# Weights that share an address between layers, one level of a scan folded into another, and loops written out

## The reference, cut to what matters

```
# layer 2, per sample (32 heads of 16), xa = layer norm of x, sx = previous token's xa - xa
xxx = tanh((xa + sx * maa_x) @ maa_w1).reshape(l, 5, 32)
xxx = einsum('lfd,fde->lfe', xxx, maa_w2)
xk, xw, xv, xr, xg = xa + sx * (maa_stack + xxx)
w = exp(-exp(time_decay + tanh(xw @ td_w1) @ td_w2))
r, k, v, g = xr @ Wr.T, xk @ Wk.T, xv @ Wv.T, silu(xg @ Wg.T)
for t: a = k_t v_t;  out_t = r_t (u * a + s);  s = a + w_t * s
x1 = x + groupnorm(out) * g @ Wo.T
x2 = x1 + sigmoid(xr2 @ Wfr.T) * (relu(xk2 @ Wfk.T) ** 2 @ Wfv.T)
# layer 3: q = x2 @ Wq, k and v from the context, softmax attention, @ Wo, layer norm
```

## Time and profile before

| | |
|---|---|
| median of 3 runs | 2489.3 us (2488.08 to 2489.41) |
| the profiled execution's own time | 2494.95 us |
| its span, first to last instruction | 2492.6 us |
| PE busy | 2331.0 us, 94% |
| DVE, ACT, POOL busy | 45%, 43%, 22% |
| mean granted PE clock | 0.966 |
| DMA | 81.93 MB, mean 33 GB/s |

### The profile page before, as it was taken

The page is one execution under the profiler, slowest core; times in us unless marked ns, Lnnn a source line. Parts: engine busy times, 40 slices in busy tenths (PEclk is TensorE's granted clock), DMA queues, the critical chain, the costliest instruction groups (busy, mean ns, idle before and its releaser), DMA issues. The chain is left out here.

```text
span 2492.6 us, 59022 instructions
## 1 busy us (share of the span) xinstructions
PE 2331.0 (94%) x22880; PEld 1720.1 (69%) x22880; DVE 1111.1 (45%) x3070; ACT 1082.6 (43%) x3409; POOL 552.4 (22%) x585
## 2 busy tenths in 40 slices
PE   7886999999999999999488999999999999999986
PEld 3444667777777666667276878777777877777864
DVE  5662222222222222222234565655666655665542
ACT  4552333333333333333112655555555455555544
POOL 0001010110000000000023334333333343343320
PEclk9997999999999999999678999999999999999998
DMA  5421000000000000000600000111000011100010
GB/s 165 168 89 65 15 18 18 22 18 18 18 18 18 18 18 18 18 10 5 191 15 16 21 17 14 25 25 25 20 20 12 23 25 25 25 20 16 10 25 14
DMA packets 117056, 81.93 MB, mean 33 GB/s; under 512 B 79136, under 2 KB 91680, under 8 KB 114720
## 3 DMA queue, kind: packets, MB, share of 16 engines
q1 hardware_dynamic: 107744, 54.32, 8.2%
q0 software_dynamic: 2240, 12.58, 1.5%
q10 hardware_dynamic: 6912, 12.59, 1.3%
HBM read 62.68 MB, written 12.58 MB: 30 GB/s over the span
## 5 line engine op out<-in xcount | busy, mean ns | idle before, releaser
L745 PEld LDWEIGHTS bank<-normedT,mlp_w 128*128 128x128 f32 x2048 | 235.7, 193 | 18.3 <-issue 17.1
L745 PE MATMUL bank<-normedT,mlp_w 128*128 128x128 f32 x2048 | 241.7, 278 | 0.8 <-DVE normedT L975 0.8
L755 PE MATMUL bank<-mlp_w,geluT 128*128 128x512 f32 x512 | 228.9, 595 | 0.0
L1638 PEld LDWEIGHTS quad<-rT,k_even_odd 32*128 32x128 f32 x6144 | 187.2, 193 | 39.5 <-DVE wkv_scores L2095 29.7
L926 DVE CUSTOM_DVE_ANT_0 probs<-quad,neg_mask 128x256 f32<-128x256 f32 x256 | 90.8, 421 | 273.8 <-PE quad L675 273.8
L1638 PE MATMUL quad<-rT,k_even_odd 32*128 32x32 f32 x6144 | 197.9, 278 | 13.9 <-DVE wkv_scores L2095 11.5
L2095 DVE COPY_PREDICATED wkv_scores<-level_masks,quad 128x1024 f32<-128x1024 int32 x96 | 160.6, 1673 | 93.4 <-PE quad L1638 93.4
L1930 ACT ACTIVATE scores<-scores,nmax 128x128 f32<-128x128 f32 x512 | 198.9, 400 | 2.9 <-DVE nmax L2185 2.9
L933 DVE COPY probsT<-quad 128x512 f32<-128x512 f32 x128 | 84.9, 683 | 191.9 <-PE quad L689 191.7
L755 PEld LDWEIGHTS bank<-mlp_w,geluT 128*128 128x128 f32 x512 | 93.6, 190 | 103.4 <-issue 103.4
L1445 POOL TENSOR_TENSOR k_even_odd<-k_even_odd,decay_products 128x512 f32<-128x512 f32 x80 | 95.9, 1199 | 275.9 <-PE quad L1638 275.9
(11 more groups left out here) (238 smaller groups left out, 4463.7 us busy)
## 6 DMA issues: line engine op xcount, KB each, us to landing
x_in<-in_x SPq DMA_DIRECT2D x32, 256.0 KB, 3.0
mlp_w<-in_mlp_w POOLq DMA_DIRECT2D x8, 1024.0 KB, 5.5
ctx_in<-in_ctx SPq DMA_DIRECT2D x16, 256.0 KB, 2.9
l_out<-wy ACTq DMA_DIRECT2D x16, 256.0 KB, 2.2
wy_in<-l_out SPq DMA_DIRECT2D x16, 256.0 KB, 3.4
hT<-in_ctxT SPq DMA_DIRECT2D x16, 256.0 KB, 3.5
l_out<-l_x ACTq DMA_DIRECT2D x16, 256.0 KB, 2.0
x_in<-l_out SPq DMA_DIRECT2D x16, 256.0 KB, 3.0
```

Source lines behind the costliest of these rows:

```text
L745: mm = nc.tensor.matmul(PS[b][:, f * P:(f + 1) * P], mlp_w1[:, c, m * P:(m + 1) * P], nT[:, c, :], start=(c == 0), stop=(c == NC - 1))
L755: mm = nc.tensor.matmul(PS[M.bank][:, :], gT[:, f, :], mlp_w2[:, f, :], start=(f == 0), stop=(f == NF - 1))
L1638: mm = nc.tensor.matmul(PS[r][:, at:at + SB], keys(rr, c, s), odd, start=True, stop=True)
```

## The change

Four things change.

1. **Shared weights.** `Wk`, `Wr`, `Wv` and the raw `Wg` get the addresses of layer 1's `q_w`, `k_w`, `v_w` and `out_w`, and SP loads them in layer 1 as soon as the last sample's output projection is done. `Wo3` gets the address of the raw `Wg` once that is reordered. The other weights are loaded by ACT's queue at the start of `layers23`. Zeros, constants, the centring of `Wv` (DVE) and the reordering of `Wg` (now POOL) move behind step 0.
2. **The bonus level.** `p_diag` goes. Level 0 computes it too: keys are `K0`, in which the odd tokens carry u and the even ones don't (`p_k0` of POOL), queries are `rm`, in which even tokens carry u (`p_ur`), 64 moving columns. The merge of level 0 takes all 64 columns by a mask with diagonal and pairs.
3. **Narrower PE blocks.** `p_t5` streams `maa_w1`'s 160 columns against z as weights, and a new block `p_t5t` turns the result by two transposes; `p_mix4` uses all four row groups and quad. Level 4 loads only the keys it needs, 32 by 32 (twice as many instructions), level 5 32 by 64, and its merge is a plain copy of half the partitions. The gate's second ACT pass goes; DVE reads PSUM for it.
4. **Loops written out** for all engines, and a new `ORDER` and `USES`.

```diff
-                for t, src in zip(early, (a["maa_w1"], a["maa_w2"][0:P], a["maa_w2"][P:2 * P], a["td_w1"], a["td_w2"])):
...
+                O = ring("o")
+                sp.wait_ge(O.free, O.read(B - 1, 2))
+                for t, n in zip((q_w, k_w, v_w, out_w), ("Wk", "Wr", "Wv", "Wg")):
+                    sp.dma_start(t[:, :, :], a[n]).then_inc(s_w2, 16)
...
             for i in range(last):
                 step(*(i - k if i >= k else None for k in range(last + 1)))
+                if i == 0:
+                    segments["after_first"]()
...
-            if name_of == "pe":
-                for i in range(last, B - 1):
...
-            else:
-                with eng.Fori(last, B - 1) as i:
...
+            for i in range(last, B - 1):
+                for b in banks.values():
+                    b.turn(i - last)
+                step(i, *(i - k for k in range(1, last + 1)))
...
-                    for c in range(NC):
-                        nc.tensor.matmul(PS[b][:, 0:P], maa_w1[:, c, 0:P], z[:, c, :], start=(c == 0), stop=(c == NC - 1))
...
+                        mm = nc.tensor.matmul(PS[b][:, 0:NM * DM], z[:, c, :], maa_w1[:, c, :], start=(c == 0), stop=(c == NC - 1))
...
+                def p_t5t(i, uses):
+
+                    u, b = uses[("p_t5t",)], BANK["p_t5t"]
+                    claim(u)
+                    pe.wait_ge(s_t5, i + 1)
+                    for k in range(2):
+                        mm = nc.tensor.transpose(PS[b][:, k * P:(k + 1) * P], t5[:, k * P:(k + 1) * P], ident[:, :])
...
+                            elif lv < 6:
+                                for b in range(SB // n):
+                                    for r in range(RG):
+                                        rr, s = slice(SB * r, SB * r + SB), HALF * bh + 2 * n * b
+                                        mm = nc.tensor.matmul(PS[r][4 * n * b:4 * n * b + 2 * n, at + n * b:at + n * b + n],
+                                                              keys(K2, rr, c, s, n), rT[rr, c, s + n:s + 2 * n], start=True, stop=True)
...
+                def p_k0(i, uses):
+
+                    u = uses[("p_k",)]
+                    pool.wait_ge(u.free, u.done)
...
+                    if lv == 0:
+                        op = nc.vector.copy_predicated(AD[:, :, :], lm[:, NLM:NLM + HALF].unsqueeze(1).to_broadcast([P, RG * NC * 2, HALF]),
+                                                       grid)
...
+                    else:
+                        op = nc.vector.tensor_copy(AD[0:HALF, :, SB:HALF], grid[0:HALF, :, 0:SB])
...
-            sp=[("p_v",), ("n_lds0",), ("w_lda",), ("n_ldx",), ("p_ldw",)])
+            sp=[("n_ldx",), ("w_lda",), ("n_lds0",), ("p_v",), ("p_ldw",)])
```

More of the change, by code:

```diff
@@ L1223, in layers23 @@
         S = {k: (sem(f"l23_{k}_psum_ready"), sem(f"l23_{k}_psum_free")) for k in ("quad", 5, 6, 7)}
-        USES = {("n_xa",): (6, 1), ("p_t5",): (6, 1), ("p_mix",): ("quad", RG), ("p_mix4",): (7, 1), ("p_u1",): (5, 1), ("p_w",):
-                (6, 1), ("p_k",): (5, 1), ("p_r",): (6, 1), ("p_v",): (5, 1), ("p_g",): (7, 1), ("p_diag",): ("quad", 1),
+        USES = {("n_xa",): (7, 1), ("p_t5",): (6, 1), ("p_t5t",): (6, 1), ("p_mix",): ("quad", RG), ("p_mix4",): ("quad", 1),
+                ("p_u1",): (6, 1), ("p_w",): (6, 1), ("p_k",): (7, 1), ("p_r",): (5, 1), ("p_v",): (7, 1), ("p_g",): (6, 1),
@@ L1559, in p_mix4 @@
                 def p_mix4(i, uses):
-                    u, b, t = uses[("p_mix4",)], BANK["p_mix4"], uses[("p_t5",)]
+                    u, t = uses[("p_mix4",)], uses[("p_t5t",)]
                     claim(u)
@@ L1605, in p_g, with keys @@
                     channel_major(uses[("p_g",)], BANK["p_g"], columns(W["Wg"]), mixed(4))
[L1607 to L1622 removed]
+                def keys(t, rr, c, s, n=HALF):
+                    return t[rr, c, s:s + n, :].rearrange("p s e -> p (s e)")
                 def p_level(i, uses, lv):
@@ L1774, in b_out @@
                     token_major(uses[("b_out",)], BANK["b_out"], W["Wo3"], rows(attnT))
-                steps(pe, "pe", dict(n_xa=n_xa, p_t5=p_t5, p_mix=p_mix, p_mix4=p_mix4, p_u1=p_u1, p_w=p_w, p_k=p_k, p_r=p_r, p_v=p_v,
-                                     p_g=p_g, p_diag=p_diag, p_level=p_level, p_s0=p_s0, p_av=p_av, p_av6=p_av6, w_var=w_var,
+                steps(pe, "pe", dict(after_first=after_first, n_xa=n_xa, p_t5=p_t5, p_t5t=p_t5t, p_mix=p_mix, p_mix4=p_mix4, p_u1=p_u1, p_w=p_w, p_k=p_k, p_r=p_r, p_v=p_v,
+                                     p_g=p_g, p_level=p_level, p_s0=p_s0, p_av=p_av, p_av6=p_av6, w_var=w_var,
                                      w_rstd=w_rstd, w_out=w_out, w_xc=w_xc, w_fk=w_fk, w_fr=w_fr, w_fv=w_fv, a_x=a_x, a_q=a_q,
@@ L1955, in b_store @@
                     act.dma_start(a["out"][i], out[:, :]).then_inc(s_store, 16)
-                steps(act, "act", dict(n_xa=n_xa, p_t5=p_t5, p_xm=p_xm, p_u1=p_u1, p_w=p_w, p_k=p_k, p_r=p_r, p_v=p_v, p_g=p_g,
+                steps(act, "act", dict(after_first=after_first, n_xa=n_xa, p_t5=p_t5, p_t5t=p_t5t, p_xm=p_xm, p_u1=p_u1, p_w=p_w, p_k=p_k, p_r=p_r, p_v=p_v, p_g=p_g,
                                        p_level6=p_level6, p_wkv=p_wkv, w_rstd=w_rstd, w_xc=w_xc, w_fk=w_fk, w_fr=w_fr,
@@ L2178, in a_max @@
                             dve.wait_ge(s_attnT, i)
+                    if k == 3 and later(i):
+                        dve.wait_ge(s_store, 16 * i + 16)
                     if k % RG == 0:
@@ L2284, in program @@
         rows1 = sb1("rows1", [P, ROWS1, D])
[L2285 to L2288 removed]
+        q_w, k_w, v_w, out_w = shared
         mlp_w1 = sb1("mlp_w1", [P, NC, NF * P])
```

358 lines of the change are left out of this document (186 added, 172 removed).

## The result

The changed kernel takes 2392.2 us in the median of four runs (2389.04 to 2394.74), beside 2489.36 (2488.08 to 2490.52) for the kernel before: a ratio of 0.9609 with the interval 0.9593 to 0.9626, so 97 us less. The profiled run took 2392.45 us.

What follows compares the result with a forecast made beforehand. PE, busy 94% of the span, was taken to bound the kernel, along with the seam into layers 2 and 3. Seam 18, step 1 5 and steps 2 to 16 75 sum to 98 us: 2391 against the median, range 2372 to 2422.

Steps and rivals of the forecast that it cites:

- diagonal: PE's work per step: dropping the block `p_diag` saves 1.94 us, with nothing added to level 0.
- t5 and its transposes: PE's work per step: 2.08 us becomes 1.07 plus 0.25 for two transposes, saving 0.76 us.
- fifth mix: PE's work per step: `p_mix4` in four row groups takes 0.28 us for 1.08, saving 0.80.
- level 5: PE's work per step: 64 matmuls with half the weight columns, 14.4 ns each, take 0.92 us for 1.92, saving 1.0.
- level 4: PE's work per step: 128 small matmuls at 11 ns take 1.41 us, saving 0.5, ends -0.3 and +1.0.
- Rival 2: Levels 4 and 5: small matmuls of one row group never go below 30 ns, 3.4 us per step worse, 2445; chance 0.08.
- Writing the loops out: Loops of all engines: costed at nothing, could bring at most 3.5 us, PE's waits in twelve steps.
- The seam: Layer 1 to layers 2 and 3: p_k of sample 0 starts earlier, gain 18 us, ends 8 and 24.
- Step 1: First step, a chain of levels partly at half clock: one level fewer and a shorter level 5, about 5 us.
- rival 3: Full steps: a new wait of 1 to 2 us in 12 to 15 steps, 2412 in the middle; chance 0.19.
- rival 4: SP's spreading of v comes late, slower once 6.5 us are lost per step; 2504 at 7.5 us; chance 0.03.
- rival 5: PE's time for the dropped parts was hidden; mixed with other rivals, a third of the gain, 2455; chance 0.08 with mixtures.

Runs made afterwards that it cites:

- SP's list changed: The changed kernel with SP's spreading of v put ahead of the loads of layer 3's inputs and of the state: 2388.47 us, ratio 0.9591.
- the trial of late weights: The changed kernel with the four shared weights loaded by SP behind the start of layers 2 and 3, not in layer 1: 2403.36 us, ratio 0.9654.

## Why the prediction was right, and where it was not

The forecast was 2391, the result 2392.2, inside the range. Its sum against the profiled execution before was 98, and the traces show 98.8 for the block. But some of its terms were off, and they cancelled: that the sums came out within 1 us is luck.

**A full step** was to be 68.4; most are 68.31 and the mean is 68.50. The terms, per step, for the steps of 68.31:

| term | forecast | measured | from |
|---|---|---|---|
| diagonal | 1.94 | 1.93 | level 0 doubled |
| t5 and its transposes | 0.76 | 0.62 | 2.08 - 1.46 in the timelines |
| fifth mix | 0.80 | 0.65 | one row group |
| level 5 | 1.0 | 0.85 | levels 4 and 5 wide, less level 4 wide |
| level 4 | 0.5 | 0.58 | level 4 wide |
| PE's wait for a merge, by the loops | 0 | 0.39 | the kernel before, written out |
| sum | 5.0 | 5.02 | 73.35 - 68.31 = 5.04 |

Without the 0.39 the five terms that the forecast did count give 4.63 for 5.0, and the longer steps take another 0.19 from the mean.

- *Small matmuls.* Three terms were scaled from blocks with more instructions or other shapes, and each came out 0.14 or 0.15 too good. Level 5 takes 1.06, 16.6 ns each, for the 14.4 of L1666, whose weights are 128 rows by 32 columns where these are 32 by 64. Level 4's choice of 11 ns held: 1.92 - 0.58 = 1.34, 10.5 ns each; with SP's list changed it is 1.19 from start to start, 9.3 each. What I had not seen is that the level makes some steps longer.
- *Rival 2*, a floor of 30 ns per matmul, is out: the 128 pairs of level 4 would have taken 3.84 us. The Trainium skill (TensorE: Matmul & The Clock Gate, "Wait — 56ns, not 53.3ns?") states about 25 ns from start to start however small the matmul. This trace does not agree for tiles of part of the array: 1.51 us from start to start, in the longest case, for 128.
- *Writing the loops out* is the step that failed. I took it at zero because "its waits are 3.5 us in twelve steps, with the others looped or, in steps 3 and 15, not". The row was right and I didn't ask why there were eleven waits of one length: eleven is the number of turns of the loop (steps 4 to 14), and step 15, outside it, took 72.97 us with no wait. The written-out kernel before shows the waits gone and 7 us less, twice the bound I gave; the bound had used the 0.3 of the list where the spacing of the starts gives 0.39, and left out all that lies outside full steps. In the changed kernel the same choice is worth 6.5 us, at another place: `b_out` has next to no room behind ACT's copy of `a_x`. I had listed the slack of the t5 transposes (0.5) and of the second score block (0.85), and neither ran out; the tightest one, a bank's release two instructions down ACT's list, I had not listed.

**The seam** was to give 18 and gave 14.6. By the prediction's own chain, measured from the first load: sample 0 took 5.76 us to the norm (1206.14 - 1200.38) where I had 3.5; norm to z 10.7 where I had 8, since L2078 took 3.41 beside POOL's memsets, for 0.52 to 0.55 elsewhere; the constants 1.96 where I had 3.7; the centring 6.7 as laid out; from there to p_k 3.2 for 3.6. Why sample 0 took 5.76 stays open. The kernel before had shown the same stretching in its own constants, its first three small instructions taking 1.55 to 1.70 us, for 0.15 to 0.27 after the change, right where POOL's memset ran (1203.46 to 1205.26), and I used the 3.6 to 4 us as if they were DVE's own:

```profile
1203.46 1.80 POOL L1383 MEMSET wkv_scores<- 128x2048 f32 x1 [36.38 <-POOLq L528]
1203.60 1.70 DVE L1974 TENSOR_SCALAR bq_scaled<-cols 128x4 f32<-128x4 f32 x1 [2.62 <-PEq L528]
1203.67 1.62 DVE L1975 TENSOR_REDUCE even_odd_head<-hsum 128x2 f32<-128x8 f32 x1
1203.74 1.55 DVE L1976 TENSOR_REDUCE eye<-ident 128x64 f32<-128x128 f32 x1
```

That the weights would no longer be waited for was right, and is the bulk of it (12.2 us). The cover of the new mix chain over the centring was not seen: I had only DVE's chain.

**Step 1** gave 7.6 for 5, and the end 6.3 for 5. Of the end, 4.6 is step 16 by the terms without the loops' wait, which that step did not have; what makes the rest of both was not tried. Part of it can be PE's granted clock, which differed in the end between the two runs of the kernel before's order (0.73 and 0.80, above). These two made up for the 3.4 us that the seam fell short, and that is luck too.

**The signs.** Steps and level 4 came as foreseen. Level 5 was to be near 0.9 and is 1.06, p_k was to come within 26 us and came after 28.29, and one wait of PE is over 0.3, the hole of 1.14.

**The other rivals.** No new wait for an engine came in full steps (rival 3); v arrived in time with SP's list as changed (rival 4): the late spreading costs level 4's 0.14 in each step, and some of the longer steps. Of rival 5 nothing is seen, since each part of the step undone by itself gives back its time, the diagonal and level 4 in the even steps.

## What to carry to other kernels

A wait that returns with one length in every turn of a loop and is missing in the steps outside it belongs to the loop, whatever engine it is put down to; count the waits against the turns, and compare a looped step with one outside it. In this kernel the loops cost PE nothing or 0.4 to 0.5 us per turn, according to what waits closely for the looped engine, at the turn or in its middle: find that engine and write it out. When weights are moved ahead of a seam, look next at who shares the first few us with the new path's first instructions: here POOL's memsets cost the critical norm 2.9 us, and a second chain of equal length hid what the first one saved.

## What the runs showed of the hardware

- **DVE beside POOL.** The same `TENSOR_SCALAR` of 128 by 512 took 0.52 to 0.55 us alone and 3.41 while POOL's four memsets ran, ending at 1211.43 where they ended at 1211.15. In the kernel before, three small instructions of DVE had ended at 1205.30, with the first memset of the four (1205.26). The four instructions of z took 1.14 alone (with POOL's copies held back in the trial of late weights), 1.86 with POOL's copies beside their first half and 4.38 with the copies beside them all along. The Trainium skill (GPSIMD Engine Reference, "1. Specifications") says that POOL shares its SBUF interfaces with VectorE, with contention for instructions in a 2-port mode or with two SBUF inputs. These rows agree as far as they go: z reads two tiles; whether the `TENSOR_SCALAR` was in a 2-port mode they do not show.
- **Who comes first.** DVE's product with two inputs, r by the decays, took 1.38 us where POOL's had started 0.06 before it and 0.43 where POOL's started 0.04 after it; POOL's then took 1.39 for 1.15.
- **A turn of a loop on ACT** costs 0.51 - 0.17 = 0.34 us before its first instruction. The Trainium skill (Runtime: NRT & Kernel Launch, "Instruction fetch mechanics") says that a branch breaks the sequential prefetch and that kernels prefer full unrolling where possible; the sign agrees, but that the 0.34 us are such a fetch is not shown.
- **A hole in dense small matmuls.** In one step of the changed kernel (the interval of 69.45 us) PE waits for no semaphore, and its weight loads stop too:

```profile
1805.93 1.03 PE L1524 MATMUL bank<-ident,scores 128*128 128x128 f32 x8 [1.14 <-issue]
```

  It stands two small blocks behind level 4, whose 128 matmuls ran from 1801.81 to 1803.13. SP's spreading of v is not what makes it: here it was issued at 1801.00 over 3.88 us, but with SP's list changed its issue was over by 1793.17, and the hole still came ahead of 1804.44, 1.03 us long. A hole of this kind came once, at 0.5 to 1.3 us, in every trial of the changed kernel with the narrow level 4 but the one that doubles level 0, and not at all in the two with level 4 wide. That it is PE's instruction fetch, which the 64 more matmuls of level 4 would strain, is an argument and was not shown.
